# Six of twelve blocks of attention probabilities turned by VectorE and transfers instead of TensorE

## The chip, the cores and the metric

The kernel runs on one core of a Trainium2 chip. The metric is the device time of one execution in microseconds (us). Before the change the median of 3 runs was 595.22 us, between 594.51 and 595.42.

## The reference

Eight sequences of 256 rows of width 256 go through half a feed-forward step, an attention step and another half feed-forward step:

```python
x = x + 0.5 * ffn(layernorm(x))
x = x + attn(layernorm(x))        # 16 query heads, 4 key heads, width 64, rotary, causal
x = x + 0.5 * ffn(layernorm(x))
# ffn(x)  = (silu(x @ w_gate.T) * (x @ w_up.T)) @ w_down.T      hidden width 1024
# attn(x): x_n = x / norm(x) * 16 * gamma;  q, k, v = x_n @ w_qkv;  rotate q, k
#          out = softmax(q @ k.T / 8, causal) @ v;   result = out @ w_out
```

All is float32 within tolerance. Matmul operands are split into a high and a low part (names ending in hi and lo), and three products (hi hi, hi lo, lo hi) stand for one.

## The kernel before, in words

One program holds a queue of work for each engine. The order in each queue is written out by hand as a list of calls, and semaphores connect the queues; an engine works strictly in order. An opening treats the first sequence, a loop of six turns follows (line 1144 on TensorE, 873 on VectorE, 586 on ScalarE, 421 on GpSimd; SyncE's is unrolled), and an ending treats the last sequence. In a turn one sequence's attention stands between gate, up and down products of two feed-forward steps, which belong to neighbouring sequences.

Attention of one sequence is worked in eight groups n = 0 to 7: two tiles of 128 query rows (t = n // 4) times four key heads. A group has the four query heads of its key head. Groups 0 to 3 see one block of 128 keys, groups 4 to 7 two (kb = 0 and 1), so there are twelve blocks of probabilities. For each group:

- SyncE restacks the rotated queries and keys by transfers of 32 partitions each (`k_restack` L257, `q_restack` L265).
- TensorE forms `scores` in two halves (L1006). ScalarE and GpSimd copy and mask those of groups 0 to 3; VectorE takes the row maximum (`mask_max` L766), ScalarE the exponentials (`exps` L522), VectorE the inverse of the sum, GpSimd multiplies (`normalise` L376, the operation at L381).
- `p_transposes(n, kb)` (L1032) turns a block so that keys stand on the partitions: four TensorE transposes of 128x128 (L937) into a PSUM bank, one for each head. Two banks serve all transposes in turn.
- ScalarE copies the bank to the high part (`p_hi` L503), VectorE subtracts to get the low part (`p_lo` L691, the operation at L685, one input in PSUM and one in SBUF), both into `p_even` or `p_odd` by the parity of n.
- `values(n)` (L1039) multiplies by the value rows. `small_half` (L533) and `add_large_half` (L792) join two halves of the result in `o_sums`, and `outputs_hi`, `outputs_lo`, `projection` follow.

`xa_t` (high and low) holds the turned attention rows of a sequence. It is read by the query, key and value products at the start of a turn and written again at the turn's end (`x_transposes("xa")`, `x_hi(xa_t)`, `x_lo(xa_t)`). `x_in` is loaded by SyncE (`x_load` L277) after its last reader in a turn, and read again at the next turn's start (`first_statistics`). Other VectorE operations that the prediction speaks of are the gate's and up's products (L812, L820), the subtraction of rotated keys (`rope_lo`, L747, both inputs in SBUF) and the layer norm's shift (L679); GpSimd's power is at L324.

## Time and profile before

| | |
|---|---|
| median of 3 runs | 595.22 us |
| the profiled execution | 594.24 us |
| its span | 592.4 us |
| granted TensorE clock, mean | 0.994 |
| TensorE, VectorE, ScalarE, GpSimd busy | 95%, 74%, 67%, 65% |

The profiled execution's time is its span and 1.8 us around it. A busy time is the union of the durations of an engine's instructions. Matmuls overlap, so what one costs is read from the start of one to the start of the next.

### The profile page before, as it was taken

Reading aid. Unit: us, or ns where it says so; the run is one execution under the profiler, and the core shown is the slowest. Engines: PE = TensorE matmul, PEld = TensorE weight load, DVE = VectorE, ACT = ScalarE, POOL = GpSimd, SP = SyncE. Lnnn points to the kernel's source line nnn. Section 1 sums busy time; section 2 is a strip of 40 time slices with the busy share of each in tenths; the row PEclk is TensorE's granted clock in tenths of the full one; section 3 lists DMA queues with packets and bytes.
Section 4 is the critical chain, followed back from the end, with each engine's and each line's share of the span. In section 5 each row is a group of like instructions: output and inputs, shape, how many; then the busy total and the mean of one; then the engine's idle time right before and its main releaser. Section 6 shows DMA issues by size and latency. Waiting matters only on the chain.

```text
span 592.4 us, 13551 instructions
## 1 busy us (share of the span) xinstructions
PE 560.4 (95%) x4308; PEld 525.4 (89%) x4308; DVE 435.9 (74%) x1302; ACT 395.0 (67%) x1045; POOL 382.4 (65%) x368
## 2 busy tenths in 40 slices
PE   6889988999999999999999999999999999988997
PEld 2877777989999999999999999999999999777897
DVE  4768886859867795868867695868867696888632
ACT  3564993479736895379826896379926896379722
POOL 0666772887739765696838875686838875476523
PEclk9999998999999999999999999999999999989999
DMA  7410000350006200260005300170004400000000
GB/s 251 141 69 3 1 1 20 83 131 2 19 19 156 56 18 0 62 169 0 18 18 134 79 18 0 41 189 0 18 18 116 96 0 0 18 2 2 1 18 19
DMA packets 28089, 29.68 MB, mean 50 GB/s; under 512 B 2976, under 2 KB 25888, under 8 KB 28064
## 3 DMA queue, kind: packets, MB, share of 16 engines
q1 hardware_dynamic: 28064, 29.37, 19.0%
q8 instruction: 13, 0.21, 0.1%
q14 instruction: 12, 0.10, 0.1%
HBM read 8.39 MB, written 2.10 MB: 18 GB/s over the span
## 4 chain that ended last, share of the span: by engine, by line
PE 59%; ACT 13%; issue 10%; DVE 8%; SPq 5%; POOL 3%; DMA 1%; POOLq 0%; DVEq 0%; ACTq 0%
PE bank L928 40%; PE bank L937 7%; PE bank L1049 5%; ACT probs L528 5%; PE bank L1027 4%; SPq L273 3%; PE bank L1023 2%; SPq L262 2%; ACT hid L555 1%; DVE hid L812 1%; PE bank L923 1%; ACT xn L464 1%; DVE rope_s L700 1%; ACT o_sums L540 1%; DMA q_t<-rotated 1%
## 5 line engine op out<-in xcount | busy, mean ns | idle before, releaser
L381 POOL TENSOR_TENSOR probs<-probs,inv_sum 128x512 f32<-128x512 f32 (+1 forms) x64 | 94.0, 1470 | 43.7 <-DVE inv_sum L789 43.5
L528 ACT ACTIVATE probs<-probs,neg_max 128x128 f32<-128x128 f32 (+1 forms) x256 | 113.1, 450 | 1.6 <-DVE neg_max L779 1.6
L390 POOL TENSOR_TENSOR hid_lo<-hid,hid_hi 128x512 fp32r<-128x512 f32 x64 | 83.8, 1314 | 22.4 <-ACT hid_hi L563 21.6
L928 PE MATMUL bank<-xf_t_hi,gate_hi 128*128 128x256 f32 x256 | 75.2, 294 | 5.3 <-DVE hid L812 2.1
L928 PE MATMUL bank<-down_hi,hid_hi 128*128 128x256 f32 x256 | 72.6, 283 | 1.9 <-POOL hid_lo L390 1.9
L928 PE MATMUL bank<-xf_t_hi,up_hi 128*128 128x256 f32 x256 | 72.1, 282 | 0.0
L400 POOL TENSOR_TENSOR o_t_lo<-o_sums,o_t_hi 128x512 fp32r<-128x512 f32 x32 | 41.8, 1305 | 46.7 <-ACT o_t_hi L547 46.6
L928 PE MATMUL bank<-xf_t_lo,gate_hi 128*128 128x256 f32 x256 | 71.6, 280 | 0.0
L928 PE MATMUL bank<-xf_t_hi,gate_lo 128*128 128x256 f32 x256 | 71.6, 280 | 0.0
L928 PE MATMUL bank<-down_lo,hid_hi 128*128 128x256 f32 x256 | 71.4, 279 | 0.0
L928 PE MATMUL bank<-down_hi,hid_lo 128*128 128x256 f32 x256 | 71.4, 279 | 0.0
L928 PE MATMUL bank<-xf_t_lo,up_hi 128*128 128x256 f32 x256 | 71.3, 278 | 0.0
L928 PE MATMUL bank<-xf_t_hi,up_lo 128*128 128x256 f32 x256 | 71.3, 278 | 0.0
L555 ACT ACTIVATE hid<-bank 128x512 f32<-128x512 f32 x64 | 38.1, 596 | 42.1 <-PE bank L928 32.2
L812 DVE SCALAR_TENSOR_TENSOR hid<-hid,bank 128x512 f32<-128x512 f32 x64 | 43.6, 682 | 27.2 <-ACT hid L555 26.7
L796 DVE TENSOR_TENSOR o_sums<-o_sums,bank 64x512 f32<-64x512 f32 x64 | 43.6, 681 | 23.5 <-ACT o_sums L540 22.9
L324 POOL TENSOR_TENSOR power_out<-power_in,exponent 128x4 f32<-128x4 f32 x24 | 27.1, 1127 | 49.6 <-DVE less_mean L649 49.6
L372 POOL TENSOR_TENSOR probs<-probs,mask_sb 128x256 f32<-128x256 f32 x64 | 46.9, 741 | 15.7 <-ACT probs L518 14.3
L928 PEld LDWEIGHTS bank<-xf_t_hi,gate_hi 128*128 128x128 f32 x256 | 48.5, 190 | 9.6 <-DVE hid L812 3.7
L540 ACT ACTIVATE o_sums<-bank 64x512 f32<-64x512 f32 x64 | 38.0, 593 | 25.6 <-PE bank L1049 23.2
L937 PE MATMUL bank<-eye_sb,probs 128*128 128x128 f32 x384 | 52.6, 273 | 1.2 <-POOL probs L381 1.2
L779 DVE CUSTOM_DVE_ANT_0 probs<-bank,probs 128x128 f32<-128x128 f32 x128 | 31.6, 286 | 27.3 <-POOL probs L372 26.8
(128 smaller groups left out, 1896.5 us busy)
## 6 DMA issues: line engine op xcount, KB each, us to landing
q_t<-rotated SPq DMA_DIRECT2D x96, 128.0 KB, 2.7
k_t<-rotated_k SPq DMA_DIRECT2D x48, 128.0 KB, 2.7
x_in<-in_x SPq DMA_DIRECT2D x7, 256.0 KB, 2.8
out<-y_out SPq DMA_DIRECT2D x7, 256.0 KB, 2.1
probs<-in_w_qkv SPq DMA_DIRECT2D x4, 384.0 KB, 3.3
probs<-in_w_gate SPq DMA_DIRECT2D x2, 512.0 KB, 6.0
probs<-in_w_up SPq DMA_DIRECT2D x2, 512.0 KB, 6.9
probs<-in_w_down SPq DMA_DIRECT2D x2, 512.0 KB, 5.7
```

The lines of the kernel that those rows point to most:

```text
L372: nc.gpsimd.tensor_tensor(part, part, mask_sb[:, SEQ - P:].unsqueeze(1).broadcast_to([P, 2, P]), ALU.add).then_inc(low_masked, 1)
L381: nc.gpsimd.tensor_tensor(part, part, inv_sum[:, slot].unsqueeze(2).broadcast_to([P, GROUP, keys]), ALU.mult).then_inc(p_done, 1)
L390: nc.gpsimd.tensor_tensor(hid_lo[:, slot].rearrange("p c n -> p (c n)"), hid[:, slot], hid_hi[:, slot].rearrange("p c n -> p (c n)").bitca ...
L400: nc.gpsimd.tensor_tensor(o_t[1][:, t, jp].rearrange("p g s -> p (g s)"), o_sums[:], o_t[0][:, t, jp].rearrange("p g s -> p (g s)").bitcas ...
L528: last = nc.scalar.activation(part, part, ACT.Exp, bias=neg_max[:, slot, g:g + 1], scale=-1.0, accum_out=row_sum[:, slot, g:g + 1])
L540: nc.scalar.activation(o_sums[rows], bank[O_BANK][other], ACT.Copy).then_inc(o_small, 1)
L555: nc.scalar.activation(hid[:, slot], bank[G_BANK][:], ACT.Tanh, scale=0.5).then_inc(th_done, 1)
L779: last = nc.vector.tensor_tensor_reduce(part, bank[S_BANKS[pair]][:, g % 2 * SEQ:g % 2 * SEQ + keys], mask_sb[:, SEQ - keys:SEQ] if second ...
L796: nc.vector.tensor_tensor(o_sums[rows], o_sums[rows], bank[O_BANK][rows], ALU.add).then_inc(o_sum, 1)
L812: nc.vector.scalar_tensor_tensor(out=hid[:, slot], in0=hid[:, slot], scalar=1.0, in1=bank[G_BANK][:], op0=ALU.add, op1=ALU.mult).then_inc( ...
L928: last = nc.tensor.matmul(dst, a[x], b[y], start=start and i == 0, stop=stop and i == 2, skip_group_check=shared)
L937: last = nc.tensor.transpose(t_bank(c)[:, i * P:i * P + P], block_in, eye_sb[:])
```

## The change

The blocks (2,0), (3,0), (4,0), (5,0), (6,0) and (7,0) of a turn of the loop no longer go through TensorE. For each, `turn_blocks` has VectorE turn every 32x32 square in place of the 128x128 block, from `probs` into one of two buffers `turned`. SyncE then sends four transfers (`z_restack`), each from 32 partitions of `turned` to 128 partitions of one half of `xa_t`, which is free at that time (`landing`). ScalarE copies from there to the high part (`turned_hi`), VectorE subtracts to the low part (`turned_lo`), now with both inputs in SBUF. Landing buffer and `turned` alternate by block, so block m waits for block m-2: `turn_blocks` for its transfers, the transfers for its subtraction.

The columns of a turned block come in another order of heads and rows (pieces of 32 rows). TensorE's transposes that remain write in that order (`by_rows`), and the halves are put back in the old order when `o_sums` is written (`head_order`). In `values` the key block kb = 1 comes first, and each block waits for its own subtraction. Opening and ending keep all their transposes. The lists of calls of the loop are written in a new order on all five engines.

```diff
-TRANSPOSES = dict(opening=22, turn=15, ending=20)
+BLOCK = 32
+TURNED = [(2, 0), (3, 0), (4, 0), (5, 0), (6, 0), (7, 0)]
+TRANSPOSES = dict(opening=22, turn=15 - len(TURNED), ending=20)
...
-        sb("under_rotated_k", [P, 2, 2, SEQ])
+        turned = sb("turned", [P, 2, P // BLOCK, GROUP * BLOCK])
...
+        def landing(m):
+
+            return xa_t[m % 2][:].rearrange("p k s -> p (k s)").bitcast(F32)
+
+        def head_order(turn, part, bank_order=False):
+
+            if turn.now is None:
+                return part
+            if bank_order:
+                return part.rearrange("p (a g q) -> p a g q", a=P // BLOCK, g=GROUP)
+            return part.rearrange("p (g a q) -> p a g q", a=P // BLOCK, g=GROUP)
...
+            def z_restack():
+
+                m = c["Z"]
+                sp.wait_ge(z_ready, turn.at(z_ready, m + 1))
+                if m == 0:
+                    sp.wait_ge(v_ready, turn.at(v_ready, 1))
+                elif m > 1:
+                    sp.wait_ge(z_lo, turn.at(z_lo, m - 1))
+                for a in range(P // BLOCK):
+                    sp.dma_start(landing(m)[:, a * P:a * P + P], turned[BLOCK * a:BLOCK * a + BLOCK, m % 2]
+                                 ).then_inc(z_in[m], 16)
+                c["Z"] += 1
...
-                k_restack(0), q_restack(0), k_restack(1), q_restack(1), k_restack(2), q_restack(2), k_restack(3)
-                q_restack(3), x_load(), y_store()
+                k_restack(0), q_restack(0), q_restack(1), k_restack(1), q_restack(2), k_restack(2), k_restack(3)
+                q_restack(3), z_restack(), z_restack(), z_restack(), z_restack(), z_restack(), z_restack(), x_load()
+                y_store()
...
+                if turn.now is not None and dst is xa_t:
+                    act.wait_ge(z_lo, turn.at(z_lo, len(TURNED)))
...
+            def turned_hi(n, kb):
+
+                m = TURNED.index((n, kb))
+                act.wait_ge(z_in[m], turn.at(z_in[m], 16 * (P // BLOCK)))
+                if n > 1:
+                    act.wait_ge(o_ready, turn.at(o_ready, GROUPS + n - 1))
+                nc.scalar.activation(p_t[n % 2][0][:, kb], landing(m), ACT.Copy).then_inc(z_hi, 1)
...
-                nc.scalar.activation(o_sums[rows], bank[O_BANK][other], ACT.Copy).then_inc(o_small, 1)
+                nc.scalar.activation(head_order(turn, o_sums[rows]), head_order(turn, bank[O_BANK][other], True), ACT.Copy
+                                     ).then_inc(o_small, 1)
...
+            def turn_blocks(n, kb):
+
+                m = TURNED.index((n, kb))
+                dve.wait_ge(p_done, turn.at(p_done, GROUPS + n + 1))
+                if m == 0:
+                    for j in range(KV_HEADS):
+                        dve.wait_ge(k_in[j], turn.at(k_in[j], 16 * 2))
+                if m > 1:
+                    dve.wait_ge(z_in[m - 2], turn.at(z_in[m - 2], 16 * (P // BLOCK)))
+                nc.vector.transpose(turned[:, m % 2].rearrange("p b (g q) -> p g b q", g=GROUP),
+                                    probs[:, n % 4, :, kb * P:kb * P + P].rearrange("p g (k b) -> p g b k", b=P // BLOCK)
+                                    ).then_inc(z_ready, 1)
+
+            def turned_lo(n, kb):
+
+                m = TURNED.index((n, kb))
+                dve.wait_ge(z_hi, turn.at(z_hi, m + 1))
+                nc.vector.tensor_tensor(p_t[n % 2][1][:, kb], landing(m), p_t[n % 2][0][:, kb].bitcast(F32), ALU.subtract
+                                        ).then_inc(z_lo, 1)
...
-                nc.vector.tensor_tensor(o_sums[rows], o_sums[rows], bank[O_BANK][rows], ALU.add).then_inc(o_sum, 1)
+                sums = head_order(turn, o_sums[rows])
+                nc.vector.tensor_tensor(sums, sums, head_order(turn, bank[O_BANK][rows], True), ALU.add).then_inc(o_sum, 1)
...
-                    last = nc.tensor.transpose(t_bank(c)[:, i * P:i * P + P], block_in, eye_sb[:])
+                    to = t_bank(c)[:, i * P:i * P + P]
+                    if by_rows:
+                        to = t_bank(c)[:].rearrange("p (a g q) -> p a g q", a=P // BLOCK, g=GROUP)[:, :, i]
+                    last = nc.tensor.transpose(to, block_in, eye_sb[:])
...
             def values(n):
 
                 t, j = n // KV_HEADS, n % KV_HEADS
-                pe.wait_ge(t_lo, turn.at(t_lo, c[f"p{n % 2}"]))
                 if n == 0:
                     pe.wait_ge(v_done, turn.at(v_done, c["V"]))
                 else:
                     pe.wait_ge(o_sum, turn.at(o_sum, c["O"]))
-                for kb in range(t + 1):
+                for kb in range(t, -1, -1):
+                    if turn.now is not None and (n, kb) in TURNED:
+                        pe.wait_ge(z_lo, turn.at(z_lo, TURNED.index((n, kb)) + 1))
+                    else:
+                        pe.wait_ge(t_lo, turn.at(t_lo, c[f"p{n % 2}"]))
                     for s in range(2):
                         last = nc.tensor.matmul(bank[O_BANK][:], v_halves[:, kb, j], p_t[n % 2][s][:, kb],
-                                                start=kb == 0 and s == 0, stop=kb == t and s == 1)
+                                                start=kb == t and s == 0, stop=kb == 0 and s == 1)
                 last.then_inc(o_ready, 1)
                 c["O"] += 1
...
+                qk(0), qk(1), qk(2), qk(3), x_transposes("ff"), qk(4), gate(), value_rows(), up(), gate(), up()
+                values(5), p_transposes(7, 1), down(), down(), values(6), projection(0, 0), values(7)
```

TensorE before, from the transposes of group 6 (kb 1 and 0) to its values:

```order
L937 MATMUL bank2<-eye_sb,probs 128x128 x3
L935 REGISTER_ALU [waits p_done]
L937 MATMUL bank3<-eye_sb,probs 128x128 [waits t_lo]
L937 MATMUL bank3<-eye_sb,probs 128x128 x3
L1049 MATMUL bank4<-p_even_hi,v_halves 128x512 [waits o_sum,t_lo]
L1049 MATMUL bank4<-p_even_lo,v_halves 128x512
L1049 MATMUL bank4<-p_even_hi,v_halves 128x512
L1049 MATMUL bank4<-p_even_lo,v_halves 128x512
```

TensorE now, the values of group 6:

```order
L1117 REGISTER_ALU [waits o_sum]
L1119 MATMUL bank4<-p_even_hi,v_halves 128x512 [waits t_lo]
L1119 MATMUL bank4<-p_even_lo,v_halves 128x512
L1115 REGISTER_ALU
L1119 MATMUL bank4<-p_even_hi,v_halves 128x512 [waits z_lo]
L1119 MATMUL bank4<-p_even_lo,v_halves 128x512
```

The transposes of block 0 are gone, those of block 1 stand further ahead, with products between them and the values, and the second pair of matmuls has a wait of its own, for the subtraction of the turned block.

VectorE before, from the sum of group 4 on:

```order
L789 RECIPROCAL inv_sum<-row_sum 128x4 [waits e_done]
L796 TENSOR_TENSOR o_sums<-o_sums,bank4 64x512 [waits o_small]
L684 REGISTER_ALU
L685 TENSOR_TENSOR p_even_lo<-bank2,p_even_hi 128x512 [waits t_hi]
L684 REGISTER_ALU
L685 TENSOR_TENSOR p_even_lo<-bank3,p_even_hi 128x512 [waits t_hi]
L796 TENSOR_TENSOR o_sums<-o_sums,bank4 64x512 [waits o_small]
L812 SCALAR_TENSOR_TENSOR hid<-hid,bank5 128x512 [waits th_done]
L820 TENSOR_TENSOR hid<-hid,bank6 128x512 [waits gate_used,u_ready]
L684 REGISTER_ALU
L685 TENSOR_TENSOR p_odd_lo<-bank2,p_odd_hi 128x512 [waits t_hi]
L796 TENSOR_TENSOR o_sums<-o_sums,bank4 64x512 [waits o_small]
```

VectorE now, from the gate's product ahead of the turning of block (6,0):

```order
L874 SCALAR_TENSOR_TENSOR hid<-hid,bank5 128x512 [waits th_done]
L744 STREAM_TRANSPOSE turned<-probs 128x4x4x32 [waits z_in2,p_done]
L850 RECIPROCAL inv_sum<-row_sum 128x4 [waits e_done]
L882 TENSOR_TENSOR hid<-hid,bank6 128x512 [waits gate_used,u_ready]
L725 REGISTER_ALU
L726 TENSOR_TENSOR p_odd_lo<-bank3,p_odd_hi 128x512 [waits t_hi]
L858 TENSOR_TENSOR o_sums<-o_sums,bank4 64x4x4x32 [waits o_small]
L751 REGISTER_ALU
L752 TENSOR_TENSOR p_odd_lo<-xa_t_lo,p_odd_hi 128x512 [waits z_hi]
L744 STREAM_TRANSPOSE turned<-probs 128x4x4x32 [waits z_in3,p_done]
L698 REGISTER_ALU
L678 BN_STATS stats<-x1_next 128x6 [waits d_used]
```

The squares of blocks (6,0) and (7,0) are turned here, and the subtraction between them, that of block (5,0), reads the landing buffer and the high part, both in SBUF, instead of a bank.

SyncE before, from the last keys' transfers to the end of a turn:

```order
L262 DMA k_t<-rotated_k 128x1x256 [waits first_lo]
L262 DMA k_t<-rotated_k 128x1x256
L273 DMA q_t<-rotated 128x1x256 [waits rot_lo]
L273 DMA q_t<-rotated 128x1x256 x3
L281 DMA x_in<-in_x 128x2x256 [waits d_used]
L291 DMA out_0<-y_out 128x2x256 [waits d_used]
```

SyncE now, from the second turned block on (the first stands ahead of it in the same form):

```order
L302 DMA xa_t_lo<-turned 128x1x128 [waits z_ready]
L302 DMA xa_t_lo<-turned 128x1x128 x3
L302 DMA xa_t_hi<-turned 128x1x128 [waits z_lo,z_ready]
L302 DMA xa_t_hi<-turned 128x1x128 x3
L302 DMA xa_t_lo<-turned 128x1x128 [waits z_lo,z_ready]
L302 DMA xa_t_lo<-turned 128x1x128 x3
L302 DMA xa_t_hi<-turned 128x1x128 [waits z_lo,z_ready]
L302 DMA xa_t_hi<-turned 128x1x128 x3
L302 DMA xa_t_lo<-turned 128x1x128 [waits z_lo,z_ready]
L302 DMA xa_t_lo<-turned 128x1x128 x3
L310 DMA x_in<-in_x 128x2x256 [waits d_used]
L320 DMA out_0<-y_out 128x2x256 [waits d_used]
```

The transfers of six blocks have come between the last queries and the load of x_in.

## Rows read from the trace of the kernel before

**Rows 1.** The page, busy us (share of the span) and instructions of engines
```profile
PE 560.4 (95%) x4308; PEld 525.4 (89%) x4308; DVE 435.9 (74%) x1302; ACT 395.0 (67%) x1045; POOL 382.4 (65%) x368
```

**Rows 2.** Busy us of the engines in the attention stretch of one turn, us from the start
```profile
core 0: us, PE busy (x) PEld busy (x) DVE busy (x) ACT busy (x) POOL busy (x), PEclk, DMA share, GB/s
265.00:299.00 34.00, 33.90 (x268) 32.71 (x269) 27.33 (x90) 28.81 (x82) 23.27 (x19) 1.00 0.03 8
```

**Rows 3.** Timeline of TensorE, the first matmul of two turns: start us, us, what
```profile
237.13 0.28 PE L928 MATMUL bank<-xa_t_hi,qkv_hi 128*128 128x256 f32 x1
...
304.72 0.28 PE L928 MATMUL bank<-xa_t_hi,qkv_hi 128*128 128x256 f32 x1
```

**Rows 4.** Timeline of TensorE around a single and a double group of transposes
```profile
273.10 0.60 PE L937 MATMUL bank<-eye_sb,probs 128*128 128x128 f32 x4
273.45 0.48 PE L1049 MATMUL bank<-p_odd_hi,v_halves 128*128 128x512 f32 x1
...
286.98 1.03 PE L937 MATMUL bank<-eye_sb,probs 128*128 128x128 f32 x8
287.77 0.36 PE L928 MATMUL bank<-xf_t_hi,gate_hi 128*128 128x256 f32 x1
287.97 0.28 PE L928 MATMUL bank<-xf_t_lo,gate_hi 128*128 128x256 f32 x1
288.09 0.28 PE L928 MATMUL bank<-xf_t_hi,gate_lo 128*128 128x256 f32 x1
```

**Rows 5.** Timeline of TensorE, two waits in the turn's first half
```profile
249.21 0.28 PE L928 MATMUL bank<-xf_t_hi,up_lo 128*128 128x256 f32 x1
249.62 0.38 PE L928 MATMUL bank<-xf_t_hi,gate_hi 128*128 128x256 f32 x1
...
265.10 0.49 PE L1023 MATMUL bank<-k_t,q_t 128*128 128x256 f32 x2 [0.35 <-DMA q_t<-rotated]
```

**Rows 6.** SyncE's timeline (issues), then the tile q_t's transfers in this turn
```profile
246.96 1.20 SPq L262 DMA_DIRECT2D k_t<-rotated_k  x2
...
260.25 2.56 SPq L273 DMA_DIRECT2D q_t<-rotated  x4
283.93 0.38 SPq L281 DMA_DIRECT2D x_in<-in_x  x1
...
DMA to landing us min/median/max: 2.6/2.7/3.0
```

**Rows 7.** A VectorE line's durations (ns min/median/max), and a stretch of VectorE's timeline
```profile
L747 DVE TENSOR_TENSOR rotated<-rotated x6: 677/678/679, 110.8 to 449.0; 128x512 fp32r<-128x512 f32 x6
...
277.12 0.68 DVE L812 SCALAR_TENSOR_TENSOR hid<-hid,bank 128x512 f32<-128x512 f32 x1
277.72 0.68 DVE L685 TENSOR_TENSOR p_odd_lo<-bank,p_odd_hi 128x512 fp32r<-128x512 f32 x1
```

**Rows 8.** Timelines of TensorE and GpSimd: scores, normalisation and values of group 7
```profile
283.32 0.65 PE L1027 MATMUL bank<-k_t,q_t 128*128 128x256 f32 x4
...
289.78 1.90 POOL L381 TENSOR_TENSOR probs<-probs,inv_sum 128x1024 f32<-128x1024 f32 x1 [1.94 <-DVE inv_sum L789]
...
297.64 0.40 PE L1049 MATMUL bank<-p_odd_hi,v_halves 128*128 128x512 f32 x1
```

**Rows 9.** VectorE and GpSimd side by side, then durations by line (ns min/median/max)
```profile
246.20 0.73 DVE L747 TENSOR_TENSOR rotated_k<-rotated_k 128x512 fp32r<-128x512 f32 x1 [0.75 <-ACT rotated_k L500]
...
246.33 1.47 POOL L324 TENSOR_TENSOR power_out<-power_in,exponent 128x4 f32<-128x4 f32 x1
...
L324 POOL TENSOR_TENSOR power_out<-power_in,exponent x24: 1007/1018/1473, 5.0 to 566.5; 128x4 f32<-128x4 f32 x24
...
L679 DVE TENSOR_TENSOR shift<-less_mean,power_out x16: 148/516/653, 7.8 to 567.5; 128x2 f32<-128x2 f32 x16
L679 DVE TENSOR_TENSOR shift<-less_mean,factor x8: 160/161/164, 40.2 to 499.8; 128x2 f32<-128x2 f32 x8
...
L685 DVE TENSOR_TENSOR p_even_lo<-bank,p_even_hi x48: 671/684/693, 66.8 to 553.1; 128x512 fp32r<-128x512 f32 x48
```

77 lines of the change are left out of this document (39 added, 38 removed).

## The prediction

> **What bounds the kernel now.** I read the page's busy times first, then the busy times by stretch of one turn of the loop, then the timelines of TensorE, SyncE, VectorE and GpSimd in that turn. TensorE is busy 95% of the span, VectorE 74% [rows 1]. A turn of the loop lasts from 237.13 to 304.72, 67.6 us, and there are six [rows 3]. TensorE hardly pauses in it: a matmul of 256 columns follows another every 0.12 us. What interrupts it is a gate that waits for the gate's product (0.41 instead of 0.12), the scores of the fourth group that wait for a transfer (0.35), and the transposes themselves [rows 4, 5]. So TensorE's own instruction stream sets the time, and work taken off it counts if nothing else becomes late. In the attention stretch from 265 to 299, VectorE is busy 27.3 of 34.0 us and GpSimd 23.3 [rows 2]; there is the danger.
>
> The profiled execution took 594.24 us (span 592.4), the median of the runs shown is 595.22. I sum against 594.24 and add 0.98 at the end. A measurement of this kernel can tell 0.2% from no change, 1.2 us: faster is below 594.0, slower above 596.4.
>
> **TensorE loses** 6 of its 12 groups of four transposes per turn. The row's duration of a transpose is pipeline time and not what it costs. By start times a lone group takes 273.10 to 273.45, 0.35 us, a double one 0.79, and the matmul behind either needs 0.20 instead of 0.12 [rows 4]. A group is thus worth 0.43 us: 6 x 0.43 = 2.6 us per turn, **15.6 us** over six turns. Opening and ending keep their transposes. Here a rule can be weighed. The Trainium skill (VectorE: DVE Perf Modes, "The three transpose paths") gives 390 ns for a TensorE transpose and 311 ns for one on VectorE of 128 columns (bf16), and its rules for authors leave a 128x128 transpose to TensorE. By its 390 ns the sum would be 24 x 0.39 x 6 = 56 us; the start times here allow 15.6.
>
> **VectorE gains** six block transposes of 512 elements per partition. No row shows one. Nearest is a one-pass operation of 128x512 from SBUF, 0.68 us long, where the next one can start after 0.60 [rows 7]. Ends: 0.3 us (if two elements go per cycle) and 1.2 us (two passes for float32). I take 0.60: 3.6 us per turn. The rule's table would, from 311 ns at 128 columns, give at most 4 x 0.31 = 1.2 us, my upper end. The subtraction behind it keeps its 0.60 us, but both inputs now lie in SBUF, where before one lay in PSUM. That matters, because VectorE and GpSimd disturb each other over such operands in this trace. A power on GpSimd takes 1.02 us mostly and 1.47 when it runs beside the VectorE subtraction of two SBUF tiles at 246.20. A shift of two SBUF inputs takes 0.52 us where GpSimd is at work and 0.16 elsewhere. The subtraction that reads PSUM never leaves 0.67 to 0.69 [rows 9]. GpSimd is busy two thirds of the stretch with operations of 1.0 to 1.9 us, so a wait until its current one ends averages up to 2/3 x 0.8 = 0.5 us; six are 3.0 us per turn. The lower end is 0. I take 0.2 each (1.2 us), because the order was written anew and a subtraction may fall between GpSimd's operations. The Trainium skill (SBUF — State Buffer, "SBUF: two separate sides") states just this lock between a VectorE operation with two SBUF inputs and a GpSimd operation that reads SBUF, each blocking the other entirely. It speaks against this change, and is the slower rival below.
>
> **SyncE gains** 24 transfers per turn. Four of this number of rows take 2.56 us to issue, 0.64 each, and one lands 2.7 us after its issue [rows 6]. A block is in place 3 x 0.64 + 2.7 = 4.6 us after its VectorE transpose. Six times 2.56 is 15.4 us of a queue that is idle from 262.8 on except for two issues, so the queue itself costs nothing. The load of x_in moves behind the six. It stood at 283.93 [rows 6] and now goes out before the last values; its reader comes at the next turn's start: nothing, with some 8 us of cover. The key transfers that change places with query transfers keep their number, so the fourth group's transfers land when they did: nothing. ScalarE exchanges one 512-wide copy for another: nothing.
>
> **The strided head order** of the sums and of TensorE's transposed writes changes no element count, with runs of 32 elements: I cost it at nothing, the upper end at 0.1 us for each of 16 operations, hidden while VectorE and ScalarE idle.
>
> **The longer way of a block.** For group 7, scores start at 283.32, its normalisation ends at 291.68 (8.4 us later), its values start at 297.64, 14.3 us after the scores [rows 8]. In the new order one up product (1.4) and the values of group 3 (0.5) stand between as well, three transpose groups go (-1.3), and the turned block is now the second half of the values (+0.5): 15.4 us. Needed are 8.4 + 0.6 (transpose) + 4.6 (transfers) + 0.5 (ScalarE) + 0.6 (subtraction) = 14.7. So 0.7 us is left, which any queue on VectorE eats. The ring of two buffers adds its own beat: transfers of block m wait until block m-2 is subtracted, 0.6 + 4.6 + 0.5 + 0.6 = 6.3 us for two blocks, about what two groups of values are apart. The late one next is therefore TensorE's wait for the subtraction inside values(5) to values(7), and everything behind it in TensorE's order waits too.
>
> **Sum.** VectorE's stretch is the measure. It has 27.3 us of work in 34.0; now 27.3 + 3.6 + 1.2 = 32.1, and an engine that works in order and waits for others keeps some idle time: I take 1.1 us, a sixth of today's 6.7. That gives 33.2 for 34.0: 0.8 us per turn gained (TensorE sheds 2.6 and gets 1.8 back as waits in the last three values). 6 x 0.8 = 4.8: 594.24 - 4.8 = 589.4, against the median **590.4 us**. Its own range, with -0.1 to 1.5 us per turn left, is 586 to 596.
>
> **Rivals.**
> - *Full gain* (chance 0.18). The new order hides the whole way, every subtraction falls clear of GpSimd, and TensorE keeps 2.6 us per turn: 595.22 - 15.6 = 579.6. For it: TensorE sets the pace now and groups 2 to 4 have slack. Against it: the 0.7 us above and the full VectorE.
> - *VectorE becomes the bound through GpSimd* (0.27), **slower**. The place is VectorE's queue from the first block transpose to values(7). At w us of wait per subtraction the stretch needs 27.3 + 3.6 + 6w even with no other idle time. At w = 0.5 this is 33.9, today's 34.0; above it the turn is longer than now. At 0.65 it is 34.8: 0.8 per turn, 4.8 in all, 600.0. At 0.8 it is 35.7, 605. A block transpose of 1.2 us does the same at w = 0 with 34.5.
> - *Given back exactly* (0.12): the waits of TensorE for the turned blocks sum to 2.6 us per turn and the time stays at 595.2. That the change doesn't do what it says (transposes remaining on TensorE) I exclude: the order of the instructions shows them gone.
>
> **Numbers.** The forecast has 0.43, full gain 0.18, no change 0.12, slower 0.27. A little of the forecast's share reaches above 594.0 and a little of the slower case ends within 0.2%, so faster 0.60, same 0.13, slower 0.27. The range that leaves out 2 in 10 goes from the full gain to a wait of about 0.7 us: 580 to 602.
>
> **What would show it.** TensorE: six groups of probability transposes per turn, and the turn shorter than 67.6 us by 0.8. Its remaining waits should be named with the subtraction of the turned blocks, in the values of groups 5 to 7. The block transpose near 0.7 us long. The new subtractions should spread from 0.68 us upward, where the PSUM ones don't. VectorE above 85% busy in the stretch. I am wrong if TensorE waits elsewhere (for scores or for gate products), if the block transposes take over 1 us, if transfers land later than 3 us, or if the subtractions never lengthen; the last would lead to the full gain.

## The result, and the profile after

| | before | after |
|---|---|---|
| median | 595.32 us | 623.74 us |
| lowest to highest | 594.51 to 596.56 (4 runs) | 622.84 to 624.30 (4 runs) |
| span of the profiled execution | 592.4 us | 622.5 us |
| granted TensorE clock, mean | 0.994 | 0.975 |

The ratio is 1.047, with a 95% interval of 1.0447 to 1.0492. The changed kernel is slower by 28.4 us; the forecast was 590.4 us, and its range ended at 602.

The page of the changed kernel, the busy row that answers to [rows 1] and the chain that ended last by engine:

```profile
PE 573.0 (92%) x4164; PEld 522.2 (84%) x4164; DVE 501.0 (80%) x1338; ACT 403.6 (65%) x1045; POOL 393.3 (63%) x368
...
issue 25%; PE 24%; POOL 21%; DVE 17%; ACT 11%; DVEq 1%; POOLq 0%; ACTq 0%
```

TensorE has 144 instructions fewer, as meant (24 transposes in each of six turns). VectorE is busy 65.1 us more, 10.9 us in each turn; the forecast had 3.6 + 1.2 us. GpSimd, which got nothing new to do, is busy 10.9 us more. Before, the chain of waits that ended last ran over TensorE for 59% of the span; now it is spread over four engines.

The first matmul of two turns, answering to [rows 3]:

```profile
320.14 0.28 PE L992 MATMUL bank<-xa_t_hi,qkv_hi 128*128 128x256 f32 x1
...
392.36 0.28 PE L992 MATMUL bank<-xa_t_hi,qkv_hi 128*128 128x256 f32 x1
```

72.2 us for one turn, where it was 67.6. Next, the stretch of this turn that begins 27.9 us after its start, as [rows 2] did (37 us long here, because the turn is longer):

```profile
core 0: us, PE busy (x) PEld busy (x) DVE busy (x) ACT busy (x) POOL busy (x), PEclk, DMA share, GB/s
348.00:385.00 37.00, 34.38 (x240) 30.90 (x238) 36.37 (x90) 28.46 (x78) 23.72 (x18) 0.95 0.22 50
```

This row is the result in one line: **VectorE is busy 36.4 of 37.0 us**. Before, it was 28.0 in a stretch of the same length. It has next to no idle time left there, so much of what it does longer makes the turn longer (half to two thirds of the block transposes' part, by runs 2 and 5 below). The three kinds of work that the forecast priced are shown by line (ns min/median/max):

```profile
L744 DVE STREAM_TRANSPOSE turned<-probs x36: 1069/1101/1135, 135.9 to 521.9; 128x512 f32<-128x512 f32 x36
...
L752 DVE TENSOR_TENSOR p_even_lo<-xa_t_hi,p_even_hi x18: 679/1369/1881, 143.4 to 525.9; 128x512 fp32r<-128x512 f32 x18
L752 DVE TENSOR_TENSOR p_odd_lo<-xa_t_lo,p_odd_hi x18: 676/827/1965, 148.4 to 529.0; 128x512 fp32r<-128x512 f32 x18
...
L430 POOL TENSOR_TENSOR o_t_lo<-o_sums,o_t_hi x32: 1285/1570/1768, 80.1 to 591.5; 128x512 fp32r<-128x512 f32 x32
...
DMA to landing us min/median/max: 2.0/2.1/2.9
```

The block transpose takes 1.10 us, not 0.60. The subtraction with both inputs in SBUF spreads from 0.68 to 1.97 us. Together these two groups of 18 take 23.6 and 20.7 us, 1.23 us on average against 0.68 with one input in PSUM [rows 9]: 0.55 us of wait each, where the forecast took 0.2. The waits are no scatter. In all six turns they are the same to a few hundredths: 0.7, 1.3, 1.2 and 0.15 us for the blocks (2,0) to (5,0), and none for (6,0) and (7,0). Each of the four subtractions finds a GpSimd operation running and ends 0.55 us after it. GpSimd's subtraction of the outputs became longer too, though nothing of it was changed. Only the transfers did as foretold: 64 KB land 2.1 us after their issue.

How a longer subtraction reaches TensorE is seen at 364 us. The first lines are VectorE's (364.66 is block (3,0), 371.09 block (4,0)), the next GpSimd's, the last TensorE's, each in its order of time:

```profile
364.66 1.96 DVE L752 TENSOR_TENSOR p_odd_lo<-xa_t_lo,p_odd_hi 128x512 fp32r<-128x512 f32 x1
366.54 0.67 DVE L858 TENSOR_TENSOR o_sums<-o_sums,bank 64x512 f32<-64x512 f32 x1
...
371.09 1.88 DVE L752 TENSOR_TENSOR p_even_lo<-xa_t_hi,p_even_hi 128x512 fp32r<-128x512 f32 x1
```

```profile
364.18 1.89 POOL L411 TENSOR_TENSOR probs<-probs,inv_sum 128x1024 f32<-128x1024 f32 x1 [2.02 <-DVE inv_sum L850]
370.53 1.89 POOL L411 TENSOR_TENSOR probs<-probs,inv_sum 128x1024 f32<-128x1024 f32 x1 [4.46 <-DVE inv_sum L850]
372.38 1.76 POOL L430 TENSOR_TENSOR o_t_lo<-o_sums,o_t_hi 128x512 fp32r<-128x512 f32 x1
```

```profile
363.36 0.28 PE L992 MATMUL bank<-xf_t_hi,gate_lo 128*128 128x256 f32 x1
364.06 1.49 PE L1094 MATMUL bank<-k_t,q_t 128*128 128x256 f32 x8 [0.43 <-DVE neg_max L840]
367.34 0.49 PE L1119 MATMUL bank<-p_odd_hi,v_halves 128*128 128x512 f32 x1 [1.79 <-DVE o_sums L858]
```

GpSimd's normalisation runs from 364.18 to 366.07. VectorE's subtraction is there from 364.66 and ends at 366.62, 0.55 us after it: it did its 0.6 us of work once GpSimd was done. The sum of the output halves (L858) stands behind it in VectorE's queue and waits along, and TensorE's next values wait 1.79 us for that sum. GpSimd itself waited 4.46 us for an inverse that VectorE, late by now, gives at 370.45. Its normalisation starts at 370.53, VectorE's next subtraction at 371.09, and the same happens again; the GpSimd operation behind it takes 1.76 us instead of 1.31.

Over the whole execution, the waits (us in total, times, longest):

```profile
POOL probs L411 <- DVE inv_sum L850: 75.4, 39, 4.5
...
PE bank L1119 <- DVE o_sums L858: 14.6, 16, 1.8
...
PEld bank L1119 <- DVE p_odd_lo L752: 14.6, 17, 2.0
```

GpSimd's wait for the inverse was 43.5 us before. By differences of start times in the turn from 248.36 to 320.14 (71.8 us) and the one of [rows 3], TensorE loses 2.5 us more over its scores, 2.0 over its values and 1.3 over its gate products, and the probability transposes give 1.8 back.

### The profile page after: what moved, and what is told of

It reads as the page before. It is cut to its first block, busy times and chain, and to the rows that moved or that the text cites. A ratio compares the mean times of both kernels' runs of the same rounds, so it can differ in the third digit from the quotient of the medians.

```text
span 622.5 us, 13497 instructions
## 1 busy us (share of the span) xinstructions
PE 573.0 (92%) x4164; PEld 522.2 (84%) x4164; DVE 501.0 (80%) x1338; ACT 403.6 (65%) x1045; POOL 393.3 (63%) x368
## 4 chain that ended last, share of the span: by engine, by line
issue 25%; PE 24%; POOL 21%; DVE 17%; ACT 11%; DVEq 1%; POOLq 0%; ACTq 0%
PE bank L992 19%; POOL probs L411 6%; POOL hid_lo L420 5%; ACT probs L568 4%; POOL probs L402 4%; POOL o_t_lo L430 3%; DVE probs L840 3%; DVE hid L874 2%; DVE o_sums L858 2%; PE bank L1004 2%; PE bank L987 2%; DVE turned L744 2%; ACT o_sums L580 1%; PE bank L1119 1%; DVE p_even_lo L752 1%
## 5 line engine op out<-in xcount | busy, mean ns | idle before, releaser
L420 POOL TENSOR_TENSOR hid_lo<-hid,hid_hi 128x512 fp32r<-128x512 f32 x64 | 87.2, 1367 | 26.5 <-ACT hid_hi L604 26.3
L992 PE MATMUL bank<-xf_t_hi,gate_hi 128*128 128x256 f32 x256 | 76.9, 301 | 5.6 <-DVE hid L874 3.8
L992 PE MATMUL bank<-down_hi,hid_hi 128*128 128x256 f32 x256 | 75.0, 293 | 1.7 <-POOL hid_lo L420 1.7
L992 PE MATMUL bank<-xf_t_hi,up_hi 128*128 128x256 f32 x256 | 74.6, 291 | 0.7
L430 POOL TENSOR_TENSOR o_t_lo<-o_sums,o_t_hi 128x512 fp32r<-128x512 f32 x32 | 48.7, 1522 | 41.6 <-ACT o_t_hi L588 41.5
L992 PE MATMUL bank<-xf_t_hi,up_lo 128*128 128x256 f32 x256 | 72.9, 285 | 0.0
L992 PE MATMUL bank<-down_lo,hid_hi 128*128 128x256 f32 x256 | 72.9, 285 | 0.0
L992 PE MATMUL bank<-xf_t_lo,up_hi 128*128 128x256 f32 x256 | 72.8, 284 | 0.0
L992 PE MATMUL bank<-xf_t_lo,gate_hi 128*128 128x256 f32 x256 | 72.2, 282 | 0.0
L992 PE MATMUL bank<-xf_t_hi,gate_lo 128*128 128x256 f32 x256 | 72.2, 282 | 0.0
L874 DVE SCALAR_TENSOR_TENSOR hid<-hid,bank 128x512 f32<-128x512 f32 x64 | 43.5, 680 | 17.3 <-ACT hid L596 17.0
L596 ACT ACTIVATE hid<-bank 128x512 f32<-128x512 f32 x64 | 38.1, 595 | 28.4 <-PE bank L992 17.3
L992 PEld LDWEIGHTS bank<-down_hi,hid_hi 128*128 128x128 f32 x256 | 50.4, 197 | 3.8 <-POOL hid_lo L420 2.5
L402 POOL TENSOR_TENSOR probs<-probs,mask_sb 128x256 f32<-128x256 f32 x64 | 46.6, 747 | 10.1 <-ACT probs L558 9.8
L992 PEld LDWEIGHTS bank<-xf_t_hi,up_hi 128*128 128x128 f32 x256 | 49.2, 192 | 4.3 <-DVE hid L882 3.4
```

Of the source, the lines that this page charges most:

```text
L402: nc.gpsimd.tensor_tensor(part, part, mask_sb[:, SEQ - P:].unsqueeze(1).broadcast_to([P, 2, P]), ALU.add).then_inc(low_masked, 1)
L420: nc.gpsimd.tensor_tensor(hid_lo[:, slot].rearrange("p c n -> p (c n)"), hid[:, slot], hid_hi[:, slot].rearrange("p c n -> p (c n)").bitca ...
L430: nc.gpsimd.tensor_tensor(o_t[1][:, t, jp].rearrange("p g s -> p (g s)"), o_sums[:], o_t[0][:, t, jp].rearrange("p g s -> p (g s)").bitcas ...
L596: nc.scalar.activation(hid[:, slot], bank[G_BANK][:], ACT.Tanh, scale=0.5).then_inc(th_done, 1)
L874: nc.vector.scalar_tensor_tensor(out=hid[:, slot], in0=hid[:, slot], scalar=1.0, in1=bank[G_BANK][:], op0=ALU.add, op1=ALU.mult).then_inc( ...
L992: last = nc.tensor.matmul(dst, a[x], b[y], start=start and i == 0, stop=stop and i == 2, skip_group_check=shared)
```

## The experiments

All times are medians. Each ratio, with its 95% interval, is to the kernel before measured beside that run on the same chip, where it took 594.5 to 595.8 us; a difference between two runs on different chips is uncertain by about that much.

**1. The lock taken away: `lo_memset`.** The low part of the six turned blocks is cleared, and so left out of the result; the instruction writes only.

```diff
-                nc.vector.tensor_tensor(p_t[n % 2][1][:, kb], landing(m), p_t[n % 2][0][:, kb].bitcast(F32), ALU.subtract
-                                        ).then_inc(z_lo, 1)
+                nc.vector.memset(p_t[n % 2][1][:, kb].bitcast(F32), 0.0).then_inc(z_lo, 1)
```

> The six subtractions for the low part of a turned block are replaced by VectorE filling the low part with zeros (left out: the low part of those six blocks). It reads nothing from SBUF, so it has nothing to contend for with GpSimd. Lock theory (the time is lost because the subtraction with two SBUF inputs waits for GpSimd's running operation and then holds it up): 605 to 613 us, 10 to 18 below the changed kernel, and GpSimd's o_t_lo back from 1.52 to 1.31 us. Turning theory (the 1.10 us block transposes fill VectorE's queue): at most 5 us less, 619 or more. Order theory (the new order of the queues is slow by itself): about 620.

598.05 us, ratio 1.0049 [1.0031, 1.0068]: 25.7 us below the changed kernel, and below the 605 to 613 expected. GpSimd's subtraction of the outputs is back to one duration:

```profile
L430 POOL TENSOR_TENSOR o_t_lo<-o_sums,o_t_hi x32: 1291/1304/1321, 80.2 to 564.7; 128x512 fp32r<-128x512 f32 x32
```

So the two engines held each other up through this one instruction. A clear is also 0.19 us shorter than an undisturbed subtraction, 6.8 us in 36 places; the rest, some 19 us or more, is the lock's.

**2. A cheap step for the block transpose: `turn_memset`**, and **3. both: `both_memset`.** The transpose is replaced by a clear of `turned` of 0.49 us (turned values left out); in the second, the low part is cleared as well.

```diff
-                nc.vector.transpose(turned[:, m % 2].rearrange("p b (g q) -> p g b q", g=GROUP),
-                                    probs[:, n % 4, :, kb * P:kb * P + P].rearrange("p g (k b) -> p g b k", b=P // BLOCK)
-                                    ).then_inc(z_ready, 1)
+                nc.vector.memset(turned[:, m % 2], 0.0).then_inc(z_ready, 1)
```

> The block transpose on VectorE is replaced by filling the same buffer with zeros (left out: the turned values themselves; transfers, copies and subtractions stay). By the opening's fill of 128x512, 0.49 us, this takes 0.6 us off each of 36 blocks. Turning theory: 20 us less, about 604. Lock theory: 4 to 8 us less, about 617, with the subtractions still up to 1.9 us long. Order theory: about 620.

> Both replacements together (left out: turned values and their low part). If turning and lock together are the cause: below 597, 27 or more under the changed kernel. If the order of the queues or the transfers' latency is: above 607.

612.26 us, ratio 1.0282 [1.0264, 1.0301], and 586.87 us, 0.9857 [0.9841, 0.9874]. The first takes off 11.5 us, which lies between the two theories (604 and 617), for 22 us less of VectorE's work. The second takes off 36.9 and is below 597, as expected if both are the cause; 25.7 and 11.5 sum to 37.2, so the two costs simply add. With both steps cheap there is a gain, but of 9.0 us and not the 15.6 that the transposes were priced at.

**4. The change's order with TensorE's transposes: `order_only`.** No block is turned by VectorE; in the change's order the six groups of transposes stand again, (2,0) behind values(1), (3,0) ahead of values(2), the others behind (n,1), with `p_hi` and `p_lo` for `turned_hi` and `turned_lo`.

```diff
-TURNED = [(2, 0), (3, 0), (4, 0), (5, 0), (6, 0), (7, 0)]
+TURNED = []
```

> The changed kernel's order of all five queues, with the six blocks turned by TensorE again (its transposes placed behind those of key block 1, and for groups 2 and 3 ahead of the next products), no block transposes, no transfers. Order theory: 610 or more, clearly slower than the kernel before. Turning and lock theories: 592 to 600, about the time before.

655.54 us, ratio 1.1009 [1.0991, 1.1028]. TensorE waits 24.3 and 24.2 us for low parts ahead of its transposes:

```profile
PEld bank L1002 <- DVE p_even_lo L724: 24.3, 24, 2.6
PEld bank L1002 <- DVE p_odd_lo L724: 24.2, 18, 1.9
```

By its expectation (610 or more) this speaks for the order theory. But run 3 has the same order and takes 586.87 us, so the order isn't slow with blocks that go by transfers. What is slow is this order with transposes through two PSUM banks, for which it wasn't made. The run is no price for the order alone.

**5. The stride: `turn_contig`.** The block transpose reads 32 columns side by side instead of every fourth; keys then come out in an order that the values don't have.

```diff
-                                    probs[:, n % 4, :, kb * P:kb * P + P].rearrange("p g (k b) -> p g b k", b=P // BLOCK)
+                                    probs[:, n % 4, :, kb * P:kb * P + P].rearrange("p g (b k) -> p g b k", b=P // BLOCK)
```

> The block transposes read probabilities at a stride of 4 elements (key 4k+b). Here each reads its 32 columns next to each other; the same number of elements is turned, and the keys come out in an order that the values do not have, so the values of six groups are sums over wrongly paired keys. Theory A (the stride makes the transpose long): 1.10 us falls to 0.5 to 0.7 us, and the time by 6 x 0.4 to 0.6 us per turn where VectorE is the path, to 612 to 617 us. Theory B (about two cycles per element whatever the stride): 1.05 to 1.10 us and 622 to 625 us as the changed kernel. I lean to B, 65 to 35.

614.44 us, ratio 1.0345 [1.0313, 1.0377], and the duration falls to 0.70 us:

```profile
L744 DVE STREAM_TRANSPOSE turned<-probs x36: 671/698/714, 134.2 to 511.9; 128x512 f32<-128x512 f32 x36
```

I had leaned to the wrong theory. The length is the stride's: with adjacent elements the transpose takes about what the one-pass operations of [rows 7] take (0.68), with a stride of four elements 1.10. 9.3 us of the loss is the stride's.

**6. The lock brought into the kernel before: `before_lock`.** Its low part of the six blocks subtracts the high part from itself (result zero, so that low part is left out). Order, transposes and banks stay.

```diff
-                lo(p_t[n % 2][1][:, kb], t_bank(c)[:], p_t[n % 2][0][:, kb])
+                hi = p_t[n % 2][0][:, kb]
+                lo(p_t[n % 2][1][:, kb], hi.bitcast(F32) if turn.now is not None and n > 1 and kb == 0 else t_bank(c)[:], hi)
```

> The kernel before, with its own order and all TensorE transposes, but the low part of the six blocks subtracts the high part from itself, so both its inputs lie in SBUF instead of one in PSUM (the low part of six blocks becomes zero and is left out). If the lock with GpSimd is what lengthened the changed kernel, those 18 subtractions of the loop's 3 turns go in this kernel too from 0.68 us to 1.0 to 1.3 us on average, GpSimd's instructions beside them become longer, and the time rises by 5 to 20 us, to 600 to 615 us. If the lengthening belonged to the changed kernel's order or to the transfers that land in those buffers, they stay at 0.68 us and the time at 595 us.

(The loop has six turns, so 36 such subtractions, not 18.) 599.93 us, ratio 1.0092 [1.0069, 1.0114]. The line, one input in PSUM and then both in SBUF:

```profile
L685 DVE TENSOR_TENSOR p_even_lo<-bank,p_even_hi x30: 675/691/692, 69.2 to 557.4; 128x512 fp32r<-128x512 f32 x30
L685 DVE TENSOR_TENSOR p_odd_lo<-bank,p_odd_hi x30: 658/684/693, 73.8 to 560.7; 128x512 fp32r<-128x512 f32 x30
L685 DVE TENSOR_TENSOR p_even_lo<-p_even_hi x18: 684/1254/1431, 141.9 to 497.3; 128x512 fp32r<-128x512 f32 x18
L685 DVE TENSOR_TENSOR p_odd_lo<-p_odd_hi x18: 676/925/1203, 143.1 to 503.4; 128x512 fp32r<-128x512 f32 x18
```

Same instruction, size and kernel, only the place of one input differs: the PSUM form never leaves 0.66 to 0.69 us. So the lengthening belongs neither to the transfers that land in the buffer nor to the new order. The last two groups take 20.2 and 16.8 us, 1.03 on average, 0.34 more each. Here it costs 4.8 us in all (5 to 20 were expected); in the changed kernel, with VectorE full, the removal was worth 25.7.

**7. VectorE's time priced: `before_turns`**, and **8. `before_contig`.** The kernel before with six block transposes per turn added behind each `p_lo(n, 0)`, of constant data, awaited by nobody: of 1.11 us each, then (side by side) of 0.70.

```diff
+                nc.vector.transpose(turned[:, n % 2].rearrange("p b (g q) -> p g b q", g=GROUP),
+                                    gate_w[0][:].rearrange("p k n -> p (k n)")[:, 0:GROUP * SEQ].bitcast(F32).rearrange(
+                                        "p (g s) -> p g s", g=GROUP)[:, :, 0:P].rearrange("p g (k b) -> p g b k", b=4))
```

> The kernel before with six block transposes per turn added on VectorE, behind each block's low part; they turn constant data and nobody waits for their result. Nothing is taken from TensorE. It prices VectorE's own time: 18 x 1.1 = 19.8 us added. If VectorE were covered by its idle 6.7 us per late stretch, the time stays below 600 us. If the order of VectorE's work makes each added microsecond count in that stretch, 605 to 615 us. From the memset kernels (18 x 0.62 us shorter gave 11.5 us, that is all of it) I expect 605 to 613 us.

> The kernel before with 36 block transposes added on VectorE as in the run before, but each reading 32 columns side by side, so 0.70 us instead of 1.10 us: 25.2 us of VectorE's time instead of 39.9, which cost 20.3 us. If every microsecond of VectorE counts half from the first on, 607.8 us. If there is a slack that is used up first (cost = all beyond it: 39.9 less 20.3 is a slack of 19.6 us), 25.2 less 19.6 gives 600.7 us. I expect 604 us; between the two they tell whether VectorE's idle time is worth 3.3 us per turn or a share.

615.46 us, ratio 1.0353 [1.0332, 1.0374], and 605.23 us, 1.0179 [1.0150, 1.0209]. The first expectation counted 18 for 36, so that its 19.8 met the measured 20.3 by accident: 39.9 us of instructions were added, and half of it came through. The second added 25.2 and cost 10.3, four tenths. The 14.7 us between them cost 10.1, seven tenths. Neither of the two simple laws holds: VectorE's time has a price from the first microsecond on, and it rises as its idle time goes. In the 37 us that begin 27.9 us after a turn's start VectorE is busy 28.0 us in the kernel before, 32.7 and 31.5 in these two, and 36.4 in the changed kernel.

**9. TensorE's time priced: `before_short`.** The kernel before with one of four transposes for each of the six blocks (three quarters of their values left out), nothing else changed.

```diff
-                transposes([probs[:, n % 4, g, kb * P:kb * P + P] for g in range(GROUP)])
+                few = turn.now is not None and n > 1 and kb == 0
+                transposes([probs[:, n % 4, g, kb * P:kb * P + P] for g in range(1 if few else GROUP)])
```

> A correction first: the loop runs 6 turns, so six blocks per turn are 36 instructions; the expectations of the runs with the lock and the added block transposes counted 18. This one: the kernel before, with only the first of the four TensorE transposes of each of the six blocks kept (three quarters of their values are left over from earlier and wrong); nothing is put on VectorE, and every order stays. It prices what freeing TensorE brings by itself. 108 transposes of the loop go, about 0.11 us each (0.43 us per four), 11.7 us. If TensorE's time is the path, 583 to 585 us. If VectorE or ScalarE follow close behind, only part of it: 587 to 592 us. I expect 584.5 us.

593.67 us, ratio 0.9978 [0.9963, 0.9994]: **1.2 us for 108 transposes**, and I had expected 10.4. Busy rows of one turn, before and here (the columns as above):

```profile
237.13:304.72 67.59, 66.62 (x542) 64.60 (x541) 51.47 (x159) 46.84 (x128) 46.99 (x44) 1.00 0.22 54
```

```profile
237.77:305.07 67.30, 66.15 (x525) 63.13 (x523) 51.48 (x159) 46.84 (x128) 47.00 (x44) 1.00 0.22 55
```

The turn is 0.3 us shorter. By start times the probability transposes take 2.9 us of it instead of 4.7, and the scores, values, up and down products take 1.3 us more, in pauses mostly too short for the profile to name what they wait for. A TensorE that is busy 95% was not the only engine that set the pace: what it no longer did, it waited.

**10. Both mis-sized terms put right: `contig_memset`.** Edits 1 and 5 together (low part and key order left out as there).

> The changed kernel with both terms that the forecast mis-sized put near where it had them: the block transposes read side by side (0.70 us each instead of 1.10; keys in a wrong order) and the low part of the six blocks cleared (0.49 us, no lock with GpSimd; low part left out). The forecast counted 0.60 and 0.88 us. If these two terms are all that was wrong, the time comes out near the forecast of 590.4 us, within 588 to 593 us; from the two runs taken apart, 598.1 less 9.3, it is 588.8 us. If a third cost of the change was missed (its order of work, the landing), it stays above 594 us.

588.86 us, ratio 0.9902 [0.9874, 0.9929]. With a transpose of 0.70 us and no lock, the changed kernel comes out near the forecast, and what it loses against the kernel before lies in these two steps. But it isn't the forecast's case. The two steps take 1.19 us per block here. The forecast's are 1.56 in the same measure: its 0.60 from one start to the next is a duration of 0.68 [rows 7], and its subtraction 0.68 and 0.2. In 36 blocks that is 13 us more of VectorE's time, and the prices of runs 7 and 8 (four to seven tenths) would add 5 to 9 us, an estimate. So at the forecast's own durations I would expect 594 to 598 us, hardly a gain, and the 590.4 isn't confirmed by this run.

**11. GpSimd does the subtraction: `lo_pool`.** Nothing is left out.

```diff
-                nc.vector.tensor_tensor(p_t[n % 2][1][:, kb], landing(m), p_t[n % 2][0][:, kb].bitcast(F32), ALU.subtract
+                pool.wait_ge(z_hi, turn.at(z_hi, m + 1))
+                nc.gpsimd.tensor_tensor(p_t[n % 2][1][:, kb], landing(m), p_t[n % 2][0][:, kb].bitcast(F32), ALU.subtract
```

> The changed kernel, with the turned blocks' low part subtracted by GpSimd instead of VectorE (nothing left out). VectorE loses six subtractions per turn (0.68 to 1.97 us each) and no longer shares a lock; GpSimd gains six of about 1.3 us, some of them between its normalisations. If the lock and VectorE's load are the cause, 585 to 600 us, that is at least 24 us below the changed kernel; GpSimd's added 7.9 us per turn give some of it back. If GpSimd becomes the path (each later normalisation 1.3 us later), 605 to 620 us. I expect 600 us.

619.44 us, ratio 1.0412 [1.0392, 1.0432], 4.3 below the changed kernel; I had expected 600. The lock is gone, but TensorE now waits for GpSimd:

```profile
PEld bank L1119 <- POOL p_even_lo L430: 18.8, 18, 1.6
PEld bank L1119 <- POOL p_odd_lo L430: 13.0, 18, 1.0
```

All 36 values that use a turned block wait. On GpSimd the step takes 1.30 us and stands between normalisations, which is the slower case named in the expectation (605 to 620).

**12. Turned blocks in the order of before: `old_order`.** Edit 3 (both steps cheap, 586.87 us) with every engine's loop in the order of before. `turned_hi` and `turned_lo` stand where `p_hi` and `p_lo` stood, the turning steps some steps earlier.

```diff
-                mask_max(0), mask_max(1), p_lo(1, 0), turn_blocks(2, 0), mask_max(0), inverse(), gate_product()
+                mask_max(1), gate_product(), mask_max(0), mask_max(1), inverse(), p_lo(1, 0), turn_blocks(2, 0), add_large_half(0)
```

> The changed kernel with both VectorE steps replaced by cheap clears (turned values and low part of six blocks left out), as in the run that took 586.9 us, but with every engine's order in the loop as in the kernel before; the turned blocks' steps stand where that block's transposes, high part and low part stood, and the block transposes a few steps earlier. If the gain of 9 us comes from the change's order, this one takes 593 to 600 us. If it comes from TensorE's freed time (and from blocks that no longer pass through PSUM), 585 to 589 us. I expect 594 us, from the run in which removing three quarters of the transposes alone brought 1.2 us.

642.74 us, ratio 1.0800 [1.0773, 1.0827], far outside both expectations.

```profile
PE bank L1114 <- DVE o_sums L855: 37.8, 28, 2.7
```

Before, TensorE's wait for this sum was 1.8 us in all. VectorE is busy 69% only: it waits 25.8 us ahead of the turning steps for blocks that GpSimd hasn't normalised yet, and 11.4 us for the high parts of turned blocks that are still under way. A block's four issues and the last landing take some 4 us, and the old order has no place for that. Turning needs an order of its own. The 56 us to run 3 aren't the price of the old order alone, since the places of the turning steps in it were chosen by hand and no other places were tried.

**13 to 15. Is part of the new order good for the kernel before? `early_a`, `early_b`, `early_c`.** The kernel before, nothing turned, with the first part of a turn in the change's order on all engines: up to the first two groups of transposes, somewhat further on TensorE and ScalarE, and much less far. Each keeps the rest in its own order.

```diff
-                qk(0), qk(1), qk(2), qk(3), x_transposes("ff"), qk(4), value_rows(), gate(), up(), gate(), up()
-                gate(), scores(0), scores(1), up(), down(), scores(0), gate(), scores(1), up(), x_transposes("ff")
+                qk(0), qk(1), qk(2), qk(3), x_transposes("ff"), qk(4), gate(), value_rows(), up(), gate(), up()
+                scores(0), scores(1), gate(), up(), down(), scores(0), scores(1), gate(), up(), scores(0)
```

> The kernel before with nothing turned and nothing left out, but on all engines the first part of a turn (up to the first two groups' probability transposes) in the change's order, and the rest in its own. If the change's order of that part is worth something by itself, 588 to 593 us. If order only pays in the stretch of the probabilities, or with the blocks that leave PSUM alone, 594 to 600 us (a seam between two orders can cost some tenths of a us per turn). I expect 593 us.

> As the run before, but TensorE's and ScalarE's new order reaches seven steps further, to the scores behind the first values. If the later part of the new order matters, it differs from the run before by more than 2 us; I expect within 2 us of it.

> As the same kernel, but the new order only reaches to the third of the down products on TensorE (17 steps) and to the second normalised rows on ScalarE (16 steps); VectorE has it for its first 10 steps. If the gain lies in the rotation and gate steps at the turn's start, it is all here already (588 to 593 us); if it lies in the scores that come earlier, nothing is here (594 to 597 us). I expect 594 us.

596.32, 599.71 and 604.58 us, ratios 1.0027 [1.0017, 1.0037], 1.0086 [1.0069, 1.0102] and 1.0172 [1.0156, 1.0189]. None is faster than the kernel before, and all three came out slower than I expected. The early part of the new order by itself brings nothing, and the other two places at which one order passes into the other cost more.

## Why the prediction was wrong, point by point

- **Block transpose, taken 0.60 us, ends 0.3 and 1.2.** Wrong size: 1.10 us, near the upper end, because of the stride of four elements, which I had not priced at all. It was nearly the rival's own condition ("A block transpose of 1.2 us does the same"). Side by side, 0.70, the value taken would nearly have held. The stride costs 9.3 us (run 5). The 311 ns that the Trainium skill (VectorE: DVE Perf Modes, "The three transpose paths") gives for 128 columns of bf16 make 1.2 us for four times as many, an estimate; measured are 1.10 with the stride and 0.70 without, so it was near here by luck.
- **Wait of the subtraction for GpSimd, taken 0.2 us, ends 0 and 0.5.** The step that failed, in its size and in the reason given for it. 0.55 us on average, beyond the upper end. I had reckoned with a chance meeting that lasts half of GpSimd's operation. In fact the two orders are fixed and the same subtractions meet the same operations in each turn. The two longest waits, 1.3 us at (3,0) and 1.2 at (4,0), stand behind a normalisation that VectorE's own inverse released half a microsecond earlier (364.18 and 370.53), so that GpSimd starts first. The reason for 0.2, that the new order might place them clear of each other, had no row behind it; it holds for the last two blocks only. In run 6, in the old order, the wait was 0.34.
- **The other half of the lock was left out.** Run 1 and run 6 show that each engine blocks the other. The Trainium skill says just that (SBUF — State Buffer, "SBUF: two separate sides"), and these runs agree with it; but only VectorE's loss was in my sum. GpSimd was held 10.9 us longer in its instructions. It also waited 32 us more for the inverse, of which the lock's removal takes 15 away (60.0 us left in run 1); the rest comes with the full VectorE. With the lock gone 25.7 us came back, for 20 us of VectorE's waits (36 x 0.55) and 6.8 of shorter instructions. That is nearly all of it, where the block transposes gave back 0.5 and 0.6 of what they were shortened by (runs 2 and 5). That the difference is GpSimd's side is likely but not shown by a run. That a rule speaks against the change is no use where its price is then taken from its low end.
- **The rival that came true** is the slower one, by its two conditions nearly at once: 1.1 us of transpose and w = 0.55. Its own formula gives 27.3 + 6.6 + 3.3 = 37.2 us for the stretch; at 34.0 as parity that is 3.2 us per turn or 19 in all, 614. Measured were 72.2 - 67.6 = 4.6 per turn, 36.4 busy in 37.0, and 624. So some 9 us lie beyond the formula even with the right sizes; no run tells what they are. The sum took a low value for both terms, and the range up to 602 let only one of them go to its end.
- **TensorE's removed transposes, 2.6 us per turn or 15.6.** The size was about right as time on TensorE: 4.65 us of transposes in a turn before, 2.39 in run 10, where little disturbs them. What was wrong was to say that TensorE's own stream sets the time. Three quarters of the saving, alone, brought 1.2 us (run 9). VectorE's time had a price of four tenths in the same kernel (run 8). The 95% hid that both engines were near the limit.
- **The sum.** The forecast's 590.4 and run 10's 588.9 are near each other by luck in part: run 10's two steps are shorter than the forecast's. TensorE's relief brings almost nothing alone, VectorE is busy 26.6 us more than before in run 10, and yet the time falls by 6. In its turn from 234.12 to 300.46 TensorE spends 2.3 us less on the probability transposes and no more on scores and values than before (6.2 and 5.8 us), so there the relief arrives. What is different there is that six blocks no longer pass through two PSUM banks and that the order was made for it. Runs 4 and 12 show that neither works without the other (655.5 and 642.7), so their shares can't be told apart with these runs. This is left open.
- **Transfers, SyncE, head order, x_in.** Right. Four issues take 2.48 us, landing 2.1 us (taken 2.7); the sum of halves in the strided order takes 0.69 as before. That the way over the transfers costs nothing holds only in the new order, as run 12 shows. The 0.7 us of slack for group 7 was no place of loss: its turned half starts 0.24 us after the matmul ahead of it (385.44 and 385.68).
- **What would show it.** Two of the signs named for being wrong came: transposes over 1 us, and TensorE waiting elsewhere, ahead of scores (0.43 at 364.06). No transfer landed later than 2.9 us, and the subtractions did lengthen. VectorE above 85% (98%) and subtractions that spread upward had been named for the forecast; both came too, and neither could tell the forecast from its slower rival. The named place, the values of groups 5 to 7, was too narrow: the waits begin at group 3 (367.34).

No version was found that beats both kernels and computes everything. Of the ones that are faster, run 3 leaves out the turned values and their low part, run 10 the low part and the order of the keys; run 9, 1.2 us faster, leaves values out too. Restoring the low part with one input in PSUM would cost at least 0.2 us more in each of 36 places (0.68 for 0.49, an estimate), and no run did so. The keys' order would have to be carried by the transfers, which wasn't tried.

## What to carry to other kernels

Before work is moved off the engine that is busiest, price a microsecond of both engines in the kernel at hand: add idle work to the receiver and take work from the giver, each alone. Here the giver's was worth a tenth and the receiver's four to seven tenths, a clear warning against giving 4.8 us per turn to VectorE, as the forecast did, to take 2.6 from TensorE. It is a warning and no law. Such prices belong to the order in which they were taken: by them run 10 should have been some 9 us slower than the kernel before, and it was 6 us faster. When an operand moves from PSUM to SBUF, an instruction that is the same by name can come to wait for another engine, and it makes that engine wait. Count both sides. Don't take the mean of the other engine's work: with fixed orders the same instructions meet in every turn, so look up which ones will, above all where your own engine starts the other.

## What was not expected of the hardware

- VectorE's transpose of 32x32 blocks, 128x512 of float32: 1.10 us when it reads every fourth element, 0.70 when it reads adjacent ones. It wasn't lengthened by GpSimd in either (1.07 to 1.14 and 0.67 to 0.71), though it reads SBUF and writes it; the shortest, 1.07 at 357.14, had a normalisation of 1.90 us beside it.
- A VectorE subtraction of two SBUF inputs next to GpSimd: 0.68 to 1.97 us; with one input in PSUM 0.66 to 0.70 in the same kernel. One that finds GpSimd at work ends 0.55 us after GpSimd's operation. GpSimd's own went from 1.30 to 1.77.
- TensorE's granted clock in the changed kernel. TensorE waited 1.79 us until 367.34, and from 369 to 372 its matmuls of 256 columns came every 0.21 us instead of 0.12:

```profile
368.80 0.29 PE L992 MATMUL bank<-xf_t_lo,up_hi 128*128 128x256 f32 x1
368.92 0.38 PE L992 MATMUL bank<-xf_t_hi,up_lo 128*128 128x256 f32 x1
369.10 0.41 PE L992 MATMUL bank<-xf_t_hi,up_hi 128*128 128x256 f32 x1
369.31 0.41 PE L992 MATMUL bank<-xf_t_lo,up_hi 128*128 128x256 f32 x1
```

```profile
370.00:372.00 2.00, 2.00 (x11) 2.00 (x10) 1.94 (x4) 1.73 (x5) 1.47 (x1) 0.50 0.30 66
```

The window (columns as above, the clock is the last but two) has the granted clock at 0.50, that is 1.2 GHz instead of 2.4. It isn't where the loss comes from: the turn from 248.36 to 320.14 has a mean clock of 1.00 and takes 71.8 us.

```profile
248.36:320.14 71.78, 67.42 (x518) 62.49 (x517) 62.15 (x165) 48.32 (x128) 48.56 (x44) 1.00 0.31 73
```
